# Issuing the first chunk's code and scale loads from ScalarE instead of SyncE, in a cross-attention and NF4 feed-forward kernel

## What is computed

```python
x = x + xattn(layernorm(x), ctx, ctx)     # q = layernorm(x), k = v = ctx
x = x + ffn(layernorm(x), gate_codes, gate_scales, up_codes, up_scales, down_codes, down_scales)

def xattn(q, k, v):                       # 8 heads of 16 channels
    qh = softmax over the head's channels ; kh = softmax over the positions
    kvs = einsum('bnhd,bnhe->bhde', kh, vh)
    return einsum('bnhd,bhde->bnhe', qh, kvs)

def ffn(x, ...):                          # W = NF4[codes] * scales, one scale for 64 inputs
    return (silu(x @ Wg.T) * (x @ Wu.T)) @ Wd.T      # 1024 -> 2752 -> 1024
```

## Time and profile before

| | us |
|---|---|
| median of 3 runs | 1600.88 |
| fastest, slowest run | 1599.01, 1602.6 |
| span of the profiled execution, first to last instruction | 1597.2 |
| PE busy in it | 1558.9 (98%) |
| DVE busy | 1051.3 (66%) |
| ACT busy | 807.6 (51%) |
| POOL busy | 73.1 (5%) |

### The profile page before, as it was taken

One profiled execution on the slowest core, in us unless ns is written; L12 is line 12 of the kernel. 1 busy time (PEld: TensorE's weight loads), 2 busy tenths in 40 slices (PEclk: granted clock), 3 DMA queues, 4 the chain that ended last, 5 costly groups with the idle time before them and its releaser, 6 DMA issues.

```text
span 1597.2 us, 20530 instructions
## 1 busy us (share of the span) xinstructions
PE 1558.9 (98%) x7296; PEld 1296.5 (81%) x7296; DVE 1051.3 (66%) x1118; ACT 807.6 (51%) x869; POOL 73.1 (5%) x107
## 2 busy tenths in 40 slices
PE   3999999999999999999999999999999999999999
PEld 3888888888888888888888888888778888888887
DVE  2999878888888888888888888875422224422221
ACT  3688756666566666556556566645311114211110
POOL 1444200000000000000000000000000000000000
PEclk8999999999999999999999999999999999999999
DMA  4444233323333333323323333326564433433440
GB/s 158 153 164 158 107 109 119 130 102 114 108 114 109 107 108 113 103 96 118 111 101 112 108 114 111 105 96 227 196 248 148 148 114 133 148 128 119 148 146 28
DMA packets 94429, 202.73 MB, mean 127 GB/s; under 512 B 5571, under 2 KB 50627, under 8 KB 90563
## 3 DMA queue, kind: packets, MB, share of 16 engines
q1 hardware_dynamic: 94402, 202.40, 36.8%
HBM read 150.99 MB, written 51.38 MB: 127 GB/s over the span
## 4 chain that ended last, share of the span: by engine, by line
PE 89%; DVE 4%; DMA 3%; issue 1%; SPq 1%; ACT 1%; DVEq 1%; POOL 0%; ACTq 0%; POOLq 0%
PE bank L1000 20%; PE bank L1001 20%; PE bank L999 20%; PE bank L1052 8%; PE bank L1053 8%; PE bank L1054 8%; DMA F<-in_x 2%; PE bank L950 1%; DVE bn L751 1%; PE bank L977 1%; DMA F<-inter_scratch 1%; DVE F L781 1%; DVE R L809 1%; DVEq L754 1%; SPq L389 1%
## 5 line engine op out<-in xcount | busy, mean ns | idle before, releaser
L540 ACT ACTIVATE F<-F 128x1024 f32<-128x1024 bf16 x504 | 491.2, 1048 | 130.5 <-DVE F L718 124.0
L999 PE MATMUL bank<-R 128*128 128x512 f32 x1376 | 535.5, 389 | 0.0
L1001 PE MATMUL bank<-R 128*128 128x512 f32 x1376 | 535.3, 389 | 0.0
L1000 PE MATMUL bank<-R 128*128 128x512 f32 x1376 | 535.3, 389 | 0.0
L999 PEld LDWEIGHTS bank<-R 128*128 128x128 f32 x1376 | 258.3, 188 | 53.9 <-DVE R L741 0.2
L1000 PEld LDWEIGHTS bank<-R 128*128 128x128 f32 x1376 | 258.3, 188 | 53.6
L1001 PEld LDWEIGHTS bank<-R 128*128 128x128 f32 x1376 | 258.3, 188 | 53.5
L663 ACT CAST R<-F 128x2816 fp32r<-128x2816 f32 x30 | 76.8, 2559 | 347.4 <-PE bank L1058 321.7
L1052 PE MATMUL bank<-R 128*128 128x512 f32 x642 | 250.0, 389 | 2.5 <-DVE R L898 2.5
L1053 PE MATMUL bank<-R 128*128 128x512 f32 x642 | 249.8, 389 | 0.0
L1054 PE MATMUL bank<-R 128*128 128x512 f32 x642 | 249.7, 389 | 0.0
(11 more groups left out here) (83 smaller groups left out, 1135.0 us busy)
## 6 DMA issues: line engine op xcount, KB each, us to landing
F<-inter_scratch SPq DMA_DIRECT2D x30, 1408.0 KB, 7.3
inter_scratch<-F SPq DMA_DIRECT2D x84, 256.0 KB, 13.7
F<-in_gu_codes SPq DMA_DIRECT2D x41, 512.0 KB, 13.2
F<-in_gu_scales SPq DMA_DIRECT2D x41, 512.0 KB
F<-in_d_codes SPq DMA_DIRECT2D x22, 512.0 KB, 14.1
F<-in_d_scales SPq DMA_DIRECT2D x22, 512.0 KB
wd_scratch<-F SPq DMA_DIRECT2D x22, 512.0 KB, 13.4
F<-in_x SPq DMA_DIRECT2D x16, 512.0 KB, 3.5
```

Source lines behind the costliest of these rows:

```text
L540: nc.scalar.activation(lines[q % LR], code7[s], ACT.Copy, bias=offset, scale=slope).then_inc(line_ready, 1)
L999: pe.matmul(dst, hi, xh[:, tb, t, :], start=(t == 0), stop=False)
L1000: pe.matmul(dst, hi, xl[:, tb, t, :], start=False, stop=False)
L1001: i = pe.matmul(dst, lo, xh[:, tb, t, :], start=False, stop=(t == HT - 1))
```

## The change

The three loads leave SP's stream and stand at the head of ACT's, before its first wait. Sources, destinations and semaphores are the same.

```diff
             load_x(Batch(0, 0))
             load_ctx(Batch(0, 0))
-            sp.dma_start(fcodes, gu_codes[0:2].rearrange("i p n -> p i n")).then_inc(fcodes_in, 16)
             load_x(Batch(0, 1))
             load_ctx(Batch(0, 1))
-            for i in range(2):
-                sp.dma_start(fscales[:, i, :], gu_scales[i].unsqueeze(1).to_broadcast([2, BLOCK, ITEM])).then_inc(fscales_in, 16)
             mixer(sp, mixer_turn, XS)
...
         @block.scalar
         def _(act):
+            act.dma_start(fcodes, gu_codes[0:2].rearrange("i p n -> p i n")).then_inc(fcodes_in, 16)
+            for i in range(2):
+                act.dma_start(fscales[:, i, :], gu_scales[i].unsqueeze(1).to_broadcast([2, BLOCK, ITEM])).then_inc(fscales_in, 16)
+
             def hi_of(n, s, c, g, par):
```

## The result

The changed kernel took 1592.11 us (median of 17 runs, 1588.04 to 1598.52), the kernel before 1599.89 us in 17 runs taken beside it. The ratio is 0.995, with a 95% interval from 0.994 to 0.9961: about 8 us faster. The forecast was 1592.9.

What follows compares the result with a forecast made beforehand. PE, busy 98% of the span, bounds the kernel, so only its waits at the start count. Gain 51.7 - 43.2 = 8.5 us, less 0.5 for the clock, is 8: 1600.88 - 8 = 1592.9 us, range 1586.5 to 1600.5.

Steps and rivals of the forecast that it cites:

- What held `x` 2: At the start, `x` 2 landed at 35.7 us behind two scale loads moving on two of 16 DMA engines; DVE idled 18.99.
- ACT's issues: Three issues added at ACT's head cost 1.9 to 4.2 us, hidden before its first exponential; ACT ready at 4.0 to 6.3.
- Rival C: ACT is held at its third issue, as SP was for 10.29 us; gain 0.5 to 4 us, 1598.5; chance 0.08.
- The shift of turns 0 and 1: Sharing the first loads lands `x` 0 1.3 us and `ctx` 0 2.5 us later; turns 0 and 1 shift by 1.8.
- Two queues in turn: Each DMA engine serves SP's and ACT's queues alternately, packet by packet; `x` 2 then lands at about 15 to 20 us.
- Rival B: Two queues are not served in turn, so `ctx` 1 lands behind both scale loads; no change, 1600.9 us; chance 0.14.
- First bound: Chain without the scales: batch 2's exponential on ACT 15.6 us earlier, DVE's next statistics 14.9 earlier; gain at most 14.9.
- The arrival of the scales: Last scale bytes, which POOL's L512 waits for: 38.6 us without losses, 43.2 with the 4.6 us loss seen before.
- 51.7 - F: Most the kernel gains when POOL waits for scales arriving at F: transposes' old end 56.14, less 4.5, less F; 8.5 us.
- The clock behind the gap: PE idles waiting for the scales and may restart at the lower clock; 0.5 us taken off the gain.
- Rival A: The scales are not late, arriving below 37 us, so the gain is 14.9 less a little: 1586.5 us; chance 0.12.
- Rival D: Slower: the contended pace lasts and the scales come later than 51.7 us; priced 4 us slower, 1605; chance 0.11.

Runs made afterwards that it cites:

- the experiment that took one low stretch away: Changed kernel plus 32 idle 128x128 transposes on PE while it waits for the late scales in the fourth turn; 1590.98 us, 0.9941 of the kernel before.

## Why the prediction was right, step by step

**What held `x` 2.** Right, and shown from both sides: with the codes alone moved the wait stays, with the scales moved in place or in time it goes, and with the scales spread over all engines it falls from 18.99 to 2.14 us. The rule on the number of engines that the prediction takes from the Trainium skill ("DMA: Bandwidth & Descriptors") stands there in the section "Why a DMA increments its semaphore by 16 and not by 1", not in the one named.

**ACT's issues.** Right in kind: 3.57 us for three, ready at 5.73, within the 4.0 to 6.3 forecast. Rival C is false for two scale loads; with three its hold is real.

**The shift of turns 0 and 1.** `x` 0 came 0.65 us later, not 1.3; `ctx` 0 at 8.26, about 2.8 later than the 5.42 at which PE had it, a little more than the 2.5 forecast. DVE reached batch 2 at 17.59, 0.9 later than its 16.70, not 1.8.

**Two queues in turn.** Rival B needed `ctx` 1 at 30 us; DVE's maximum of batch 1 ran at 14.85 without a wait for a transfer. B is false as it was put. That the engines alternate packet by packet isn't shown directly, only that the sum made on it holds to 2.3 us.

**First bound.** ACT's exponential at 27.91 (28.3 forecast), DVE's statistics at 27.99 (28.2). Right.

**The arrival of the scales.** 40.89 against 43.2. The sum without losses was 38.6, so the losses were 2.3 us and not the 4.6 that I carried over from before. The step "with the same loss as before" was mis-sized, on the careful side.

**51.7 - F.** 10.8 at F = 40.9; the transposes ended 10.1 us early. The difference is these transposes themselves at the lower clock, 1.97 instead of 1.1. In the kernel with one more load it held to 0.1 us at the transposes, and not beyond them.

**The clock behind the gap.** I took off 0.5 us. Between the transposes and the third `kvs` the lead fell from 10.1 to 58.60 - 50.83 = 7.8 us (58.60 being the start of that row before): 2.3 us, and 0.9 in the transposes. At this row the term "I take 0.5 us off" was too small by 2.7. Rows of the kernel before:

```profile
58.60 1.88 PE L977 MATMUL bank<-F,kvs 128*128 128x512 f32 x4
...
182.47 0.48 PE L999 MATMUL bank<-R 128*128 128x512 f32 x1
```

Behind it 0.7 us came back, since the kernel before had its own low stretch at 68.00 and the changed one had none there: at the first product of the feed-forward the lead was 182.47 - 173.98 = 8.5 us. In the feed-forward 0.6 went again, to 7.9 at the end. Nothing here explains that, and it is less than two executions of one kernel differ by.

So the median was met to 0.8 us and the span to 0.1 because errors cancelled: the scales came 2.3 us earlier than forecast, the low clock took 2.7 us more, and some of that came back. A span of a single execution can't bear out 0.1 us either. The mechanism was right; the closeness is luck. One small wait I hadn't named: DVE idled 2.53 us for `x` 4 at 38.36; that load too shares the two engines with the scales, which is likely the reason. It was covered by the longer wait.

Rival A is false for this kernel, but its condition held when the loads were spread. Rival D, slower, didn't come. The prediction let the loss begin at F = 51.7; the experiment with one more load was already 2.9 us slower than before at F = 50.6, and its trace lost the time in the low clock behind the transposes. So it begins earlier, less than 9.7 us of scale transfer away from the changed kernel.

## What to carry to other kernels

When a transfer's issue lasts many times the usual, look at what stands ahead of it and at the DMA share beside the rate: here a plateau at a share of 0.13 was two engines at work and fourteen idle. Moving such a load to another queue moves its delay to whoever waits for it, so work out that arrival as well as the one that gets free; reordering in the same queue may do as much, and spreading the load did more here than either. After a gain at the head, count what the lower clock behind the new gap takes, and follow the lead to the end of the stage: in the experiment that took one low stretch away, another stood in the next turn.

## What the runs showed of the hardware that was not expected

Spread over all engines, loads that read one 4 KB row again and again did not reach the ordinary rate. Two stretches of the kernel with spread loads on SP:

```profile
2.00:10.00 8.00, 3.67 (x17) 3.31 (x17) 2.79 (x5) 2.81 (x5) 1.64 (x6) 1.00 0.98 377
10.50:16.50 6.00, 3.29 (x15) 2.82 (x14) 3.19 (x7) 3.85 (x6) 0.74 (x2) 1.00 1.03 207
```

The engines are fully busy in both, at 377 GB/s in ordinary loads and 207 in the stretch with the scales: an estimate of 5 us for the 1 MB, in place of the 2.5 that I had put down. On SP the load of `x` 2 follows directly; in the kernel with the spread loads issued later nothing is queued behind them until 21 us, and it moved 212 GB/s at a share of 1.00 in 15 to 18.5 us. Whether the repeated reading of one row is the cause, here and for the contended pace before, was not tried by itself.

An issue can return long before its transfer is through. On ACT two scale loads were let go after 3.10 us, a third kept ACT until 18.97, and on SP the load behind two of them was held 10.29 us. The same 1 MB of scales ahead of it, but spread over all engines, held it 0.59 us. This fits that what an engine pays for an issue depends on how much is queued ahead of it on the most loaded DMA engine; how much it takes wasn't tried.
